# Middle stage of an adaLN attention and mixture-of-experts block: the normalisation moved from VectorE to ScalarE, routing weights taken from the exponentials, the row modulation placed last in VectorE's step

## The reference, cut to what matters

```python
x = x + ga * attention(h, ...)             # projection and bias inside
h = _layernorm(x, axis=-1) * (1 + cb) + sb # x1 -> xn -> rows
logits = h @ gate_w.T
scores = softmax(logits)                   # 8 per row
topk_w, topk_i = top_k(scores, 2)
topk_w = topk_w / (topk_w.sum(-1, keepdims=True) + 1e-20) * 2.5
```

## Time and profile before

| | |
|---|---|
| median of 3 runs | 3438.6 us (3434.52 to 3441.14) |
| the profiled execution's own time | 3415.04 us |
| its span | 3413.2 us |
| PE busy in the span | 2933.9 us (86%) |
| DVE busy | 2577.0 us (76%) |
| ACT busy | 1558.7 us (46%) |
| POOL busy | 879.7 us (26%) |

### The profile page before, as it was taken

The page is one execution under the profiler, slowest core; times in us unless marked ns, Lnnn a source line. Parts: engine busy times, 40 slices in busy tenths (PEclk is TensorE's granted clock), DMA queues, the critical chain, the costliest instruction groups (busy, mean ns, idle before and its releaser), DMA issues. The chain is left out here.

```text
span 3413.2 us, 71032 instructions
## 1 busy us (share of the span) xinstructions
PE 2933.9 (86%) x22564; PEld 1632.4 (48%) x22564; DVE 2577.0 (76%) x4840; ACT 1558.7 (46%) x2096; POOL 879.7 (26%) x1098
## 2 busy tenths in 40 slices
PE   5885479999898999989899997883999999788888
PEld 3553123333233333323233323773888888677776
DVE  3885788889888898888898851776677777566666
ACT  1443046666666666666666674110444444211111
POOL 1775001110111110111101111566233223233333
PEclk7998579999999999999999998775999999899999
DMA  2676311211121111212111103665555445322222
GB/s 69 184 201 175 77 28 49 55 35 48 47 54 51 42 44 47 52 47 56 39 44 47 47 6 79 202 210 174 157 157 162 150 156 159 103 93 92 92 92 74
DMA packets 385921, 315.60 MB, mean 92 GB/s; under 512 B 112636, under 2 KB 372200, under 8 KB 385640
## 3 DMA queue, kind: packets, MB, share of 16 engines
q1 hardware_dynamic: 373352, 278.44, 28.6%
q0 software_dynamic: 12288, 33.57, 2.9%
HBM read 194.27 MB, written 116.92 MB: 91 GB/s over the span
## 5 line engine op out<-in xcount | busy, mean ns | idle before, releaser
L871 ACT ACTIVATE probs<-ps_s 128x1024 f32<-128x1024 f32 (+3 forms) x1280 | 1078.0, 895 | 676.1 <-PE ps_s L1030 675.6
L895 DVE TENSOR_REDUCE piece_rest<-ps_m 128x1 f32<-128x512 f32 (+3 forms) x1344 | 800.2, 647 | 107.3 <-PE ps_m L1005 48.8
L895 DVE TENSOR_REDUCE piece_late<-ps_m 128x1 f32<-128x512 f32 (+2 forms) x960 | 587.0, 667 | 66.6 <-PE ps_m L1005 35.7
L1030 PE MATMUL ps_s<-q_st,k_st 50*128 50x512 bf16 (+7 forms) x5120 | 596.3, 347 | 37.1 <-issue 17.1
L1045 PE MATMUL ps_o<-probs,vs 128*32 128x512 f32 (+3 forms) x5120 | 605.1, 545 | 11.2 <-POOL probs L851 9.9
L851 POOL TENSOR_SCALAR_AFFINE_SELECT probs<-probs 128x256 f32<-128x256 f32 x512 | 205.0, 406 | 1551.8 <-ACT probs L871 1547.7
L996 PE MATMUL ps_m<-k_st,q_st 48*128 48x512 bf16 (+3 forms) x2560 | 451.4, 366 | 163.8 <-DVE piece_rest L895 78.6
L996 PEld LDWEIGHTS ps_m<-k_st,q_st 48*128 48x128 bf16 x2560 | 114.7, 93 | 784.4 <-DVE piece_rest L895 386.8
L1030 PEld LDWEIGHTS ps_s<-q_st,k_st 50*128 50x128 bf16 (+1 forms) x5120 | 224.3, 95 | 269.0 <-ACT probs L871 97.3
L1753 ACT ACTIVATE act_g<-ps_g 128x512 f32<-128x512 f32 x117 | 70.0, 599 | 279.1 <-PE ps_u L1845 279.1
L1790 DVE TENSOR_TENSOR hid_f<-act_g,ps_u 128x512 f32<-128x512 f32 x117 | 80.5, 688 | 126.4 <-ACT act_g L1753 126.4
(11 more groups left out here) (226 smaller groups left out, 5005.9 us busy)
## 6 DMA issues: line engine op xcount, KB each, us to landing
qk_parts<-parts SPq DMA_DIRECT2D x128, 192.0 KB, 2.8
k_st<-qk_parts SPq DMA_DIRECT2D x768, 32.0 KB, 1.8
q_st<-qk_parts SPq DMA_DIRECT2D x768, 32.0 KB, 1.8
x_r<-expert_rows SPq DMA_DIRECT2D x39, 512.0 KB, 4.4
expert_made<-made SPq DMA_DIRECT2D x39, 512.0 KB, 2.9
x_in<-in_L_attn_x_dram SPq DMA_DIRECT2D x32, 512.0 KB, 5.2
v_ones<-v_out SPq DMA_DIRECT2D x64, 256.0 KB, 4.6
vs<-v_ones SPq DMA_DIRECT2D x64, 256.0 KB, 3.8
```

Of the source, the lines that this page charges most:

```text
L871: act.activation(probs[:, u % PSLOTS, 2 * pair:2 * pair + 2, j * P:ST], ps_s[:, pair, :, j * P:ST], ACT.Exp, scale=SCALE).then_inc(exp_don ...
L895: v.tensor_reduce(dst, ps_m[:, bank, 0:n * w].rearrange("p (n w) -> p n w", n=n), AX.X, ALU.max) \
L1030: last = pe.matmul(ps_s[:, pair, z, j * P:ST], k_st[rows, slot, half, pair, kc * P:(kc + 1) * P], q_st[rows, slot, half, pair, qt * ST + j ...
```

## The change: norm on ScalarE, no scores, modulation last

ScalarE makes `xn = rstd * x1 + shift` with four `Identity` activations of 256 columns, with a scale and a shift per row; VectorE makes the shift `-mean * rstd` for it, one operation on 4 columns, between `locate` and `less_maximum`. In ScalarE's step the four stand behind the exponentials and ahead of the `h2` copies, and wait for the shift and for `scaled` of the supertile before. `rz` and `sc` are gone: the best two are taken from `ex`, and the weights are `best / (best1 + best2 + 1e-20 * z)`, which is the same quotient. The two operations of 1024 columns that make `rows` come behind `choose(u)`. GpSimd's `rstd` now waits until ScalarE has read the one before. A semaphore is saved by counting the memset of `zeros` on `pool_own`; one of the last stage, which nobody used, is gone.

```diff
@@ middle_stage, gpsimd @@
+                    pool.wait_ge(pool_own, u + 5)
+                    pool.wait_ge(x1_read, u + 3)
                     pool.tensor_tensor(rstd[:, :], var[:, :], power[:, :], ALU.pow).then_inc(rstd_done, 1)
@@ middle_stage, scalar @@
                     act.activation(ex[:, :, :], lg[:, :, :], ACT.Exp).then_inc(ex_done, 1)
                 if has(1):
+                    act.wait_ge(shift_done, u + 2)
+                    if not (isinstance(u, int) and u < 0):
+                        act.wait_ge(scale_done, u + 1)
+                    for t in range(TPS):
+                        last = act.activation(xn[:, t, :], x1[:, (s + 1) % 2, t, :], ACT.Identity,
+                                              bias=shift[:, t:t + 1], scale=rstd[:, t:t + 1])
+                    last.then_inc(x1_read, 1)
                     act.wait_ge(h2_stored[(s + 1) % 2], b * 32 + (16 * ((s + 1) // 2) + 16))
@@ middle_stage, vector @@
-            def normalise(u, slot, rslot, b):
+            def shifts(u):
                 v.wait_ge(rstd_done, u + 1)
-                for t in range(TPS):
-                    last = v.tensor_scalar(xn[:, t, :], x1[:, slot, t, :], mv[:, t, 0:1], rstd[:, t:t + 1],
-                                           ALU.subtract, ALU.mult)
-                last.then_inc(x1_read, 1)
+                v.scalar_tensor_tensor(shift[:, :], mv[:, :, 0], -1.0, rstd[:, :], ALU.mult, ALU.mult) \
+                    .then_inc(shift_done, 1)
+
+            def modulate(u, rslot, b):
                 v.wait_ge(x1_read, u + 1 + 2)
                 v.tensor_tensor(scaled[:, :, :], xn[:, :, :], cb_row[:, ds(b, 1), :].to_broadcast([P, TPS, D]),
                                 ALU.mult).then_inc(scale_done, 1)
@@ choose @@
-                step(v.tensor_reduce(z[:, :], ex[:, :, :], AX.X, ALU.add))
-                step(v.reciprocal(rz[:, :], z[:, :]))
-                step(v.tensor_tensor(sc[:, :, :], ex[:, :, :], wide(rz[:, :]), ALU.mult))
-                stand_alone(v, held)
+                v.tensor_reduce(z[:, :], ex[:, :, :], AX.X, ALU.add)
                 for t in range(TPS):
-                    last = v.max(best[:, t, :], sc[:, t, :])
+                    last = v.max(best[:, t, :], ex[:, t, :])
                 step(last)
...
-                step(v.tensor_scalar(s2[:, :], s2[:, :], 1e-20, None, ALU.add))
+                step(v.scalar_tensor_tensor(s2[:, :], z[:, :], 1e-20, s2[:, :], ALU.mult, ALU.add))
@@ run @@
                 if has(-1):
                     locate(u - 1, (s - 1) % RSLOTS)
+                if has(1):
+                    shifts(u + 1)
                 if has(0):
                     less_maximum(u)
+                    choose(u)
                 if has(1):
-                    normalise(u + 1, (s + 1) % 2, (s + 1) % RSLOTS, b + (s + 1) // SPB)
-                if has(0):
-                    choose(u)
+                    modulate(u + 1, (s + 1) % RSLOTS, b + (s + 1) // SPB)
```

More of the change, by code:

```diff
@@ L1155, in middle_stage @@
         z = sb("z", [P, TPS])
-        rz = sb("rz", [P, TPS])
-        sc = sb("sc", [P, TPS, E])
+        shift = sb("shift", [P, TPS])
         best = sb("best", [P, TPS, 8])
@@ L1210, in middle_stage @@
         rstd_done = sem("p3_rstd")
+        shift_done = sem("p3_shift")
         turned = sem("p3_turned")
@@ L1228, in middle_stage @@
         tables_in = sem("p3_tables")
-        zeroed = sem("p3_zeroed")
         step_done = sem("p3_step")
@@ L1233, in middle_stage @@
         IN_DMAS = 1 + GPB
-        ROUTE = 11
+        ROUTE = 8
         LOCATE = 4
@@ L1277, in _ @@
             sp.wait_ge(planned, 1)
-            sp.wait_ge(zeroed, 1)
+            sp.wait_ge(pool_own, 1)
             for e in range(E):
@@ L1289, in _ @@
         def _(pool):
-            pool.memset(zeros[:, :, :].rearrange("p t d -> p (t d)"), 0.0).then_inc(zeroed, 1)
+            pool.memset(zeros[:, :, :].rearrange("p t d -> p (t d)"), 0.0).then_inc(pool_own, 1)
             pool.memset(power[:, :], -0.5).then_inc(pool_own, 1)
-            pool.wait_ge(pool_own, 1)
+            pool.wait_ge(pool_own, 2)
             pool.wait_ge(consts, 48)
             pool.memset(top_row[:, :], 0.0).then_inc(pool_own, 1)
-            pool.wait_ge(pool_own, 2)
+            pool.wait_ge(pool_own, 3)
             pool.memset(top_row[0:1, :], 1.0).then_inc(biased, 1)
@@ L1323, in run @@
                     pool.tensor_scalar(var[:, :], mv[:, :, 1], EPS, None, ALU.add).then_inc(pool_own, 1)
-                    pool.wait_ge(pool_own, u + 4)
+                    pool.wait_ge(pool_own, u + 5)
+                    pool.wait_ge(x1_read, u + 3)
                     pool.tensor_tensor(rstd[:, :], var[:, :], power[:, :], ALU.pow).then_inc(rstd_done, 1)
@@ L1449, in choose @@
                 for t in range(TPS):
-                    last = v.max_index(which[:, t, :], best[:, t, :], sc[:, t, :])
+                    last = v.max_index(which[:, t, :], best[:, t, :], ex[:, t, :])
                 step(last)
@@ L1948, in shared_stage @@
         first_done = sem("p5_first")
-        mixed = sem("p5_mixed")
         summed = sem("p5_summed")
```

## The result

The changed kernel takes 3417.65 us (median of 5 runs, 3412.99 to 3421.77) beside 3434.52 us for the kernel before on the same chip (5 runs, 3434.05 to 3441.14): a ratio of 0.9949, 95% interval [0.9932, 0.9965], 17 us faster. I had forecast 3443.2 us, and a range down to 3434. The forecast was wrong in its sign.

The account below looks back on a forecast made before the run. TensorE was taken to bound the running pipeline, VectorE following, with `rows` on the path at the end. Steps 0, loop jump +1, end +3.6 gave +4.6 us: 3419.6 against the profiled execution, 3443.2 us as median, range 3434 to 3457.

Parts of the forecast that it names:

- the transfer to the median: Whole kernel: the profiled execution's 23.6 us below the median was put unchanged on the changed kernel, 3419.6 becoming 3443.2 us.
- the term of +3.6 us for the end: End of the middle stage: `rows` twice behind `choose`, so last scatters and zeros come later; +3.6 us, bounds +3 and +5.
- VectorE's saving: Each middle-stage step: 1.8 us less VectorE work, costed at nothing while TensorE sets the pace.
- the activations: ScalarE's four new operations per step: 2.0 us together, bounds 1.37 and 3.1, hidden behind `choose`.
- the lead of `rows`: Running pipeline: `rows` complete 1.9 us before TensorE takes it up, 4.2 before the change, so eleven of twelve steps cost 0.
- `locate` to `rows`: End of the stage: 7.9 us from `locate` to complete `rows`, before 5.75 and 6.05; then 6.7 us to the next `locate`.
- the two terms of my sum: Middle stage: +1 us where the loop jumps back, and 3.4 us by which the zeros come later at the end.
- the stall at the jump: Where the rolled loop jumps back: VectorE's 6.4 us idle was kept; +1 us, bounds -1.9 (stall gone) and +3.
- Rival A: TensorE's transposes in every step: VectorE becomes the bound and TensorE waits for `rows`; 19 us more, 3462 us; chance 0.12.
- Rival B: ScalarE's norm pass exposed at the end: 2.0 in place of 1.4 us, twice 0.7 us; 3444.6 us; chance 0.10.
- Rival C: Steps after the loop's jump: VectorE's relief pays, 1.4 us in each of five; 3435 us, in all twelve 3425; chance 0.12.
- Rival D: ScalarE's middle stage: `Identity` and `Exp` share no table, two loads of 1.283 us a step; 3447 us; chance 0.04.

Follow-up runs that it names:

- r1: The kernel before, unchanged, timed and profiled again: 3433.04 us, ratio 1.0003.
- r10: The changed kernel without GpSimd's scatters, the expert stage reading the input instead: 3404.20 us, ratio 0.9894 to the kernel before.
- r9: The kernel before without GpSimd's scatters, the expert stage reading the input instead: 3406.69 us, ratio 0.9908.
- r3: The kernel before with only the order changed, norm and modulation behind `choose` but still on VectorE: 3443.67 us, ratio 1.0038.
- r4: The kernel before with only the routing edit, weights taken from the exponentials, `rz` and `sc` gone: 3416.95 us, ratio 0.9961.
- r5: The kernel before with weights taken from the exponentials, but reciprocal and scores still issued, unread: 3440.49 us, ratio 0.9996.
- r6: The kernel before with weights from the exponentials and one unread VectorE addition of 128x512 per step behind `z`: 3436.25 us, ratio 0.9984.
- r8: The changed kernel with two unread VectorE additions behind `rows` in each step, about 1.8 us planned: 3416.35 us, ratio 0.9927 to the kernel before.
- r2: The changed kernel, unchanged, timed and profiled again: 3418.27 us, ratio 0.9957 to the kernel before.
- r11: The kernel before with each scatter replaced by a plain write of the same tile on the same queue, expert stage reading the input: 3408.22 us, ratio 0.9909.
- r13: The kernel before with each supertile's scatters issued one step later, right behind `rstd`: 3447.37 us, ratio 1.0042.

## Why the prediction was wrong

**The step that failed** is the transfer to the median: "It is 23.6 us faster than the median of 3438.6, and I put the same difference on the median". I took that difference as something outside the change. It sits in the middle stage (21.6 us of it, r1), in steps in which TensorE's results arrive late, and it is what the change acts on. The trace that I read has none of them: none in the running pipeline, none at the end. By W without the scatters the changed kernel loses 6 us to them, the kernel before some 25. Against typical executions the term of +3.6 us for the end was wrong too: the end takes 48.0 us in the changed kernel and 48.8 in r1. I should have seen that a profiled execution outside the spread of the timed ones, by more than any part of the change was worth, cannot stand for them.

**The steps against the trace** held almost to the tenth. VectorE's saving 1.77 us a step (1.8); the activations 2.07 us (2.0), 590 ns each; the lead of `rows` 1.8 us in the step shown (1.9); `locate` to `rows` 7.80 us (7.9), then 6.70 (6.7). In r10 against r9, the pair without disturbance, W is 3.2 us longer, where the two terms of my sum that W holds were 1 and 3.4 us. The first was too high: the part up to the transposes of u=13 takes 223.9 us in r9 and 223.8 in r10, since the stall at the jump is gone (5.7 us in r9, none in r10). I had kept that stall whole, with its loss as the lower bound.

**Rival A** did not occur: TensorE waited for `rows` twice, both times at the end. r3 shows how near it is: with the order alone there were seven such waits more, of up to 1.0 us, and the kernel was 11 us slower than before. **Rival B** was right in what it says of ScalarE, 2.07 us in place of 1.37, but the pass was hidden even at the end, where it was over at 2348.38 and its reader began at 2349.49 us. **Rival C**, that VectorE "held TensorE up in a way that the waits don't show", at 0.12, had the sign, and r4 against r5 and r6 bears it out in the old order; but r8 gave the load back in the new order and lost nothing, so VectorE's relief is at most a part of it. Its argument against (the transposes waited for nothing) was true of the trace and beside the point: their results, not their starts, are late. Its prices, 3435 and 3425 us, counted only VectorE's saved time and not the wait and the fall of the clock that follow a late end. **Rival D**: no table load in the stage.

**What stays open.** Why TensorE's results are late beside indirect scatters; whether they end late or their signal does; and whether plain writes that took as long would do the same. Why the trace first shown was free of it, with the scatters in it. And why the changed kernel has fewer late steps in the running pipeline (1 against 5 to 7), where scatters run beside the transposes in twelve steps of either kernel: there W up to the transposes of u=13 is 231.5 us in r2 and 245.1 in r1, nearly all of the gain. r4 against r5 and r6 says that in the old order 0.6 us of VectorE's time decides, r8 against the changed kernel says that in the new order three times as much, behind `rows`, doesn't. What is shown is that the difference is in these late steps, that it goes with the scatters, and at the end of the stage by which spacing.

## What to carry to other kernels

Before a sum is made on a profiled execution, set its time beside the spread of the timed ones. If it lies outside, look for what the typical execution has and this one has not, or take a second profile: that one step was worth more here than all the others. Where a wait names no releaser ("remote") and the producer's record ended long before, look at what ran beside it; leaving it out once is a quick test. When something is put in its place, as in r11, look whether the new one still runs at the same time. And a small relief of an engine with time to spare may pay more than its own time: r4 gained some 13 us by 0.6 us a step.

## What the runs showed of the hardware that I had not expected

- Beside GpSimd's indirect scatters, results of TensorE reached their consumers late while its instructions were issued on time: the ranks at the end 1.7 us, the logits behind the transposes up to 3.8 us (r5), and once, with 16 scatters in a row, the ranks 10.6 us (r13). Of 166 steps with a scatter beside the transposes 42 were late, of 58 without one none.
- Plain writes of the same tiles on the same queue did nothing of the kind (W 271.1 us against 293.9), but they were issued in 4.4 to 4.8 us a step and stood beside the transposes in three steps only.
- The same kernel shows this in some executions and, once, not at all: 3415.04 us beside 3423.7 to 3446.9 us.
- One late result can cost more than its delay. In r1 the logits at 2226.09 us, behind such transposes, ran at a granted clock of 0.50 and took 3.58 us where they take 1.95 us at 1.00 (2223.70 in the first trace).
- An activation of 128x256 with two operands per row took 590 ns on ScalarE, 64 times over.
